# The column term of the attention logits as two more columns of the q product, with the q tiles ahead of the exponentials

## What is computed

```python
h = maximum(layernorm(x), 0)                       # 512 x 256
Xw = h @ Wv + bv
sj = Xw @ aw[:256]; si = Xw @ aw[256:]             # one number per node each
e = leaky_relu(sj[None, :] + si[:, None] + ab, 0.2)
alpha = adj * exp(e)
T = alpha / (sum(alpha, -1) + 1e-12)
out = relu(h@Wk0 + T h@Wk1 + T T h@Wk2 + biases)   # q = h @ Wk2 is made first
```

## Time and profile before

| | |
|---|---|
| median of 3 runs | 1858.39 us (1857.15 to 1858.89) |
| profiled execution: its span | 1856.2 us |
| median less the profiled span | 2.2 us |
| mean granted clock of PE | 0.924 of 2.4 GHz |
| turns with both halves | 15 |

### The profile page before, as it was taken

One profiled execution on the slowest core, in us unless ns is written; L12 is line 12 of the kernel. 1 busy time (PEld: TensorE's weight loads), 2 busy tenths in 40 slices (PEclk: granted clock), 3 DMA queues, 4 the chain that ended last, 5 costly groups with the idle time before them and its releaser, 6 DMA issues.

```text
span 1856.2 us, 27152 instructions
## 1 busy us (share of the span) xinstructions
PE 1539.5 (83%) x9334; PEld 1185.5 (64%) x9334; DVE 1339.2 (72%) x3050; ACT 787.7 (42%) x1271; POOL 274.1 (15%) x167
## 2 busy tenths in 40 slices
PE   4587988979798898988989898897989789798855
PEld 3486665757667575766757676675767667576632
DVE  5666868777686877768687776868767686876623
ACT  2224436353453635335353533535353363534432
POOL 1101120111202011120201112020111201012010
PEclk9788999989899898989989898998989899898977
DMA  5013131132313203231320323123031312313030
GB/s 158 12 52 80 52 100 65 38 78 73 90 51 97 67 34 79 73 90 51 86 78 34 79 73 90 51 73 91 23 90 63 101 51 61 83 43 80 22 81 11
DMA packets 80806, 125.52 MB, mean 68 GB/s; under 512 B 10176, under 2 KB 29184, under 8 KB 80768
## 3 DMA queue, kind: packets, MB, share of 16 engines
q1 hardware_dynamic: 80768, 125.02, 24.0%
HBM read 66.27 MB, written 8.39 MB: 40 GB/s over the span
## 4 chain that ended last, share of the span: by engine, by line
PE 56%; DVE 16%; issue 13%; ACT 6%; POOL 5%; SPq 2%; DMA 1%; DVEq 0%; POOLq 0%; ACTq 0%
PE ring_f L1023 32%; PE ring_b L1023 16%; DVE att L969 6%; PE pv_acc L1289 2%; PE ring_f L1179 1%; POOL xp_s L445 1%; POOL xf L428 1%; POOL xf L426 1%; PE ring_f L1209 1%; DVE rows L898 1%; ACT att L596 1%; DVE rows L879 1%; PE ring_f L1121 1%; ACT uz L472 1%; DVE hf L850 1%
## 5 line engine op out<-in xcount | busy, mean ns | idle before, releaser
L1023 PE MATMUL ring_f<-m,inc_n 128*128 128x256 f32 x2048 | 324.2, 288 | 17.0 <-POOL m L418 14.4
L969 DVE TENSOR_TENSOR att<-ring_b,at 128x1024 f32<-128x1024 f32 x256 | 299.2, 1216 | 31.1 <-PE ring_b L1023 30.5
L575 ACT ACTIVATE att<-att 128x1024 f32<-128x1024 f32 x256 | 263.7, 1066 | 100.3 <-DVE att L969 94.4
L1023 PEld LDWEIGHTS ring_f<-m,inc_n 128*128 128x128 f32 x2048 | 289.2, 194 | 25.4 <-issue 21.0
L1023 PE MATMUL ring_b<-stk_c,stk_p 96*128 96x512 f32 x512 | 183.7, 477 | 61.1 <-DMA stk_c<-xc_s 44.5
L1023 PE MATMUL ring_f<-m,inc_t 128*128 128x256 f32 x1024 | 210.3, 284 | 14.5 <-DVE m L728 14.5
L1023 PE MATMUL ring_f<-w,uz 128*128 128x256 f32 (+1 forms) x896 | 188.1, 333 | 13.0 <-DVE uz L721 8.4
L1023 PEld LDWEIGHTS ring_b<-stk_c,stk_p 96*128 96x128 f32 x512 | 97.7, 217 | 147.3 <-issue 70.1
L407 POOL TENSOR_TENSOR rstd_f<-var_f,mhalf 128x4 f32<-128x4 f32 x48 | 48.5, 1010 | 933.2 <-DVE var_f L715 933.2
L1023 PEld LDWEIGHTS ring_f<-w,uz 128*128 128x128 f32 x896 | 151.6, 191 | 34.0 <-DVE uz L721 14.8
L1023 PEld LDWEIGHTS ring_f<-m,inc_t 128*128 128x128 f32 x1024 | 160.4, 191 | 17.7 <-DVE m L728 17.7
(11 more groups left out here) (163 smaller groups left out, 2656.7 us busy)
## 6 DMA issues: line engine op xcount, KB each, us to landing
stk_p<-xp_s SPq DMA_DIRECT2D x192, 128.0 KB, 2.4
stk_c<-xc_s SPq DMA_DIRECT2D x192, 128.0 KB, 2.3
rows<-in_adjT SPq DMA_DIRECT2D x16, 1024.0 KB, 5.3
adj_n<-in_adj SPq DMA_DIRECT2D x16, 1024.0 KB, 8.5
at<-in_adjT SPq DMA_DIRECT2D x16, 1024.0 KB, 5.2
x_in<-in_x SPq DMA_DIRECT2D x16, 512.0 KB, 3.5
out_x<-xb SPq DMA_DIRECT2D x16, 512.0 KB, 2.9
wrow<-in_adj SPq DMA_DIRECT2D x16, 256.0 KB, 6.0
```

Source lines behind the costliest of these rows:

```text
L575: act.activation(v, v, ACT.Tanh).then_inc(tanh_made.sem, 1)
L969: dve.tensor_tensor(att[:, u % 2, 2 * half:2 * half + 2], pair(tile)[:], at[:, t].unsqueeze(1).broadcast_to([P, 2, N]), ALU.mult)\
L1023: ins = pe.matmul(dst, lhsT, rhs, start=(first and n == 0), stop=(last and n == len(pairs) - 1), skip_group_check=True)
```

## The change

It does three things. The column term no longer comes from VectorE: two columns (the vector and 0.2 times the vector) are put behind the 256 of `wq`, so that each q tile has two more columns that hold si for its 128 nodes, and VectorE adds a constant pair `cst2` to them (128x2, from PSUM). The q tiles stand ahead of sj in the numbering and on PE, and their copies and subtractions ahead of the exponentials on ScalarE and VectorE. The set-up makes the two columns from a product of 2 columns in place of a row of 256.

```diff
-        wq = sb("wq", [P, 2, DT, D], F32R)
+        wq = sb("wq", [P, 2, DT, D + 2], F32R)
...
-        T_M, T_U, T_CONV, T_ZT, T_XW, T_M2, T_Y, T_HT, T_SJ, T_Q, T_TT, T_R, T_X2 = (
-            0, 2, 4, 8, 12, 14, 16, 18, 20, 21, 25, 29, 31)
+        T_M, T_U, T_CONV, T_ZT, T_XW, T_M2, T_Y, T_HT, T_Q, T_SJ, T_TT, T_R, T_X2 = (
+            0, 2, 4, 8, 12, 14, 16, 18, 20, 24, 25, 29, 31)
...
                 if i == 0:
-                    act.wait_ge(si_made.sem, si_made.after(g, 2))
+                    act.wait_ge(si_made.sem, si_made.after(g, NT))
...
-                step(dve.tensor_copy(v2_bc[:], ring_b[1][:, 0, 0:D]))
+                for c in range(DT):
+                    step(dve.tensor_copy(v2_c[:, c, 0:1], ring_b[1][:, 0, 2 * c:2 * c + 1]))
+                    step(dve.tensor_scalar(v2_c[:, c, 1:2], ring_b[1][:, 0, 2 * c:2 * c + 1], SLOPE, None, ALU.mult),
+                         now=True)
+                split(wq[:, 0, :, D:D + 2], wq[:, 1, :, D:D + 2], v2_c[:])
...
-            def f_si(g):
-
-                dve.wait_ge(h_made.sem, h_made.after(g, 2))
-                for i in range(NT):
-                    ins = dve.scalar_tensor_tensor(rows[:, i, 0:D], hf[:, i], 1.0, v2_bc[:], ALU.mult, ALU.mult,
-                                                   accum_out=si[:, 0, i:i + 1])
-                dve_f.link(ins)
-                here(dve_f, g)
-                dve.tensor_scalar(si[:, 0], si[:, 0], cst, None, ALU.add).then_inc(si_made.sem, 1)
-                dve.wait_ge(si_made.sem, si_made.after(g, 1))
-                dve.tensor_scalar(si[:, 1], si[:, 0], SLOPE, None, ALU.mult).then_inc(si_made.sem, 1)
...
                 dve.wait_ge(hi_made.sem, hi_made.after(g, H_Q + i + 1))
+                dve.tensor_tensor(si[:, i], ring_f[tile % 3][:, D:D + 2], cst2[:], ALU.add).then_inc(si_made.sem, 1)
...
-                products(ps[:, 0:D], pairs).then_inc(full.sem, 1)
+                products(ps[:, 0:D + 2], pairs).then_inc(full.sem, 1)
...
-                    (1, k_xc), (0, f_m2), (0, f_y), (1, k_scores, 0), (0, f_hT), (1, k_scores, 1), (0, f_sj),
-                    (0, f_q, 0), (1, k_attend, 0), (1, k_scores, 2), (1, k_attend, 1), (1, k_scores, 3),
-                    (1, k_attend, 2), (1, k_scores, 4), (0, f_q, 1), (0, f_q, 2), (1, k_attend, 3), (0, f_q, 3),
+                    (1, k_xc), (0, f_m2), (0, f_y), (1, k_scores, 0), (0, f_hT), (1, k_scores, 1), (0, f_q, 0),
+                    (0, f_q, 1), (1, k_attend, 0), (1, k_scores, 2), (0, f_q, 2), (0, f_q, 3), (0, f_sj),
+                    (1, k_attend, 1), (1, k_scores, 3), (1, k_attend, 2), (1, k_scores, 4), (1, k_attend, 3),
```

More of the change, by code:

```diff
@@ L139, in graph_layers @@
         b2_bc = sb("b2_bc", [P, D])
-        v2_bc = sb("v2_bc", [P, D])
+        v2_c = sb("v2_c", [P, DT, 2])
         ident = sb("ident", [P, P])
+        cst2 = sb("cst2", [P, 2])
         prm = sb("prm", [P, 24])
@@ L152, in graph_layers @@
         dn = sb("dn", [P, NT])
-        si = sb("si", [P, 2, NT])
+        si = sb("si", [P, NT, 2])
         rs = sb("rs", [P, NT])
@@ L211, in graph_layers @@
         z_made = Signal(sem("z_made"), NT)
-        si_made = Signal(sem("si_made"), 2)
+        si_made = Signal(sem("si_made"), NT)
         max_made = Signal(sem("max_made"), NT)
@@ L221, in graph_layers @@
         drained_b = Signal(sem("drained_b"), 20)
-        dve_f = Chain(sem("dve_f"), 18)
+        dve_f = Chain(sem("dve_f"), 17)
         dve_b = Chain(sem("dve_b"), 6)
@@ L252, in graph_layers @@
         SET_FIRST = 25
-        SET_DONE = 42
+        SET_DONE = 48
         BE_LINK = 5
@@ L520, in f_exp @@
                 if i == 0:
-                    act.wait_ge(si_made.sem, si_made.after(g, 2))
+                    act.wait_ge(si_made.sem, si_made.after(g, NT))
                     act.wait_ge(full.sem, full.after(g, T_SJ + 1))
-                act.activation(rows[:, i], ring_f[T_SJ % 3][:], ACT.Exp, bias=si[:, 0, i:i + 1], scale=1.0)
+                act.activation(rows[:, i], ring_f[T_SJ % 3][:], ACT.Exp, bias=si[:, i, 0:1], scale=1.0)
                 if i >= 2:
                     act.wait_ge(max_made.sem, max_made.after(g, i - 1))
-                act.activation(exp_s(i), ring_f[T_SJ % 3][:], ACT.Exp, bias=si[:, 1, i:i + 1],
+                act.activation(exp_s(i), ring_f[T_SJ % 3][:], ACT.Exp, bias=si[:, i, 1:2],
                                scale=SLOPE).then_inc(exp_made.sem, 1)
@@ L688, in set_up_rest @@
                     split(v1[:, 0, c], v1[:, 1, c], ring_b[0][:, 1, c * P:(c + 1) * P])
-                step(dve.tensor_copy(v2_bc[:], ring_b[1][:, 0, 0:D]))
+                for c in range(DT):
[3 more added lines that the diff above has]
+                split(wq[:, 0, :, D:D + 2], wq[:, 1, :, D:D + 2], v2_c[:])
                 step(dve.tensor_scalar(cst, pv_acc[:, 0:1], ab_c, None, ALU.add), now=True)
-                step(dve.tensor_tensor(cst, pv_acc[:, 1:2], cst, ALU.add))
+                step(dve.tensor_tensor(cst2[:, 0:1], pv_acc[:, 1:2], cst, ALU.add), now=True)
+                step(dve.tensor_scalar(cst2[:, 1:2], cst2[:, 0:1], SLOPE, None, ALU.mult))
                 assert n_set[0] == SET_DONE, n_set[0]
@@ L1004, in turn @@
                     (0, f_xw, 0), (1, k_keep), (0, f_xw, 1), (0, f_m2), (1, k_xc), (0, f_y), (0, f_stats2),
-                    (0, f_norm1), (1, k_unit, 0), (0, f_si), (0, f_hT), (1, k_unit, 1), (0, f_alpha, 0), (0, f_q, 0),
-                    (1, k_unit, 2), (0, f_alpha, 1), (1, k_unit, 3), (0, f_alpha, 2), (1, k_unit, 4),
-                    (0, f_alpha, 3), (0, f_sums), (0, f_q, 1), (0, f_trans), (0, f_q, 2), (0, f_q, 3), (0, f_tt),
+                    (0, f_norm1), (1, k_unit, 0), (0, f_hT), (1, k_unit, 1), (0, f_q, 0), (0, f_q, 1),
+                    (1, k_unit, 2), (0, f_q, 2), (0, f_q, 3), (0, f_alpha, 0), (1, k_unit, 3), (0, f_alpha, 1),
+                    (0, f_alpha, 2), (1, k_unit, 4), (0, f_alpha, 3), (0, f_sums), (0, f_trans), (0, f_tt),
                     (1, k_unit, 5), (-1, f_stats0), (1, k_unit, 6), (1, k_unit, 7), (-1, f_norm0), (0, f_r, 0),
@@ L1041, in set_up @@
                                                                for f in range(DT)])
-                products(ring_b[1][:, 0, 0:D], [(xp_n[:, 3, f * P:(f + 1) * P], wvt[:, f]) for f in range(DT)])
+                for c in range(DT):
+                    products(ring_b[1][:, 0, 2 * c:2 * c + 2], [(wvt[:, f, c * P:(c + 1) * P], xp_n[:, 3, f * P:f * P + 2])
+                                                                for f in range(DT)])
                 products(pv_acc[:, 0:2], [(ones, bva)]).then_inc(set_pe, 1)
@@ L1187, in f_sj @@
             def f_sj(g):
-                if not seen(g, 1):
-                    pe.wait_ge(set_dve, SET_DONE)
                 ps = bank(g, T_SJ)
                 for c in range(DT):
-                    pe.wait_ge(drained.sem, drained.after(g, drained_at(T_HT + c)))
                     v = slice(c * N, (c + 1) * N)
@@ L1197, in f_q @@
             def f_q(g, i):
+                if i == 0 and not seen(g, 1):
+                    pe.wait_ge(set_dve, SET_DONE)
                 ps = bank(g, T_Q + i)
+                if i == 0:
+                    pe.wait_ge(drained.sem, drained.after(g, drained_at(T_HT + 1)))
                 pairs = []
```

8 lines of the change are left out of this document (4 added, 4 removed).

## The result

The changed kernel takes 1892.49 us (1890.83 to 1896.57, 4 runs), before 1858.64 in the same session: ratio 1.0185, 95% interval 1.0172 to 1.0197, slower by 34 us. The profiled execution has a span of 1889.0 us, 32.8 more than before, at a mean granted clock of 0.907 (0.924 before).

A forecast was written before the change was run, and what follows sets the result against it. In the rewritten stretch PE led the chain of waits, then mostly VectorE. Delay 1.84 plus clock fall 2.2 minus give-back 0.8 made 3.2 us a turn, over 15 turns +49 us: 1907 us, range 1847 to 1916.

The forecast's parts named there:

- the forecast itself: The main case for the whole kernel's time: 1895 to 1916 us, chance 0.54.
- clock holds: Rival: no further clock fall, the delay remains; 0.3 to 1.8 us a turn, 1863 to 1885 us, chance 0.18.
- the third fall: One more drop of PE's clock each turn, just ahead of the dense work at 961.2, costing 2.2 us a turn.
- the give-back: Turns of another length lie otherwise against the clock's falls; 0.8 us a turn subtracted, ends 0 and 1.8.
- the first turn: Without a back graph, its q tiles ahead of sj cost about what the row sums saved; taken as 0.
- The row sums are covered: Row sums (1.86 us of VectorE a turn) are not in the chain; PE runs scores 1 meanwhile.
- sj comes late: Behind the q tiles on PE, sj is full at 947.8 instead of 943.46, and the exponentials wait for it.
- The division 1.84 us later: VectorE's balance for the end of L898: -1.86 +0.40 +0.70 +2.60 = +1.84 us a turn.
- the thin one: PE stretch between the attends, such as 953.4 to 956.8, busy only 1.4 of 3.4 us, ahead of a clock fall.
- turns of 111 to 113.5 us: Sign expected in the trace after: length of a turn, where settled turns took 109.23 us.
- Faster: Rival: VectorE stays the one bound of the stretch, its waiting does not grow; 1831 to 1847 us, chance 0.14.
- Absorbed: Rival: turns settle at 109.23 us again, the delay is paid once or twice; 1857 to 1862 us, chance 0.08.

The follow-up runs named there:

- no_row_sums: The kernel before, its order kept, without the four row products of the column term (that sum is left out); 1855.76 us, ratio 0.9979.
- order_only: The changed kernel's order with the old arithmetic: four row sums on VectorE again, q with 256 columns; 1913.79 us, ratio 1.0288.
- warm_no_row_sums: The kernel before with 48 idle matmuls a turn in PE's three holes and without the four row products; 1816.49 us, ratio 0.9769.
- after_filled: The changed kernel with 18 idle matmuls a turn in the holes that the q tiles left on PE; 1883.46 us, ratio 1.0127.
- dense_4: The kernel before with 4 idle matmuls a turn in a dense stretch of PE, ahead of the m2 products; 1859.86 us, ratio 0.9999.
- dense_16: The kernel before with 16 idle matmuls a turn in a dense stretch of PE, ahead of the m2 products; 1876.54 us, ratio 1.0090.

## Why the prediction was right, step by step

The direction and its cause held, and 1892.5 us lies in the range of 1847 to 1916. It lies just under the 1895 to 1916 of the forecast itself, between it and the rival "clock holds", and my value was 15 us too high. Four terms were mis-sized, and in part they cancel: over the program the delay came out 5 us smaller than I had it, the third fall 26 smaller, the give-back 9 smaller, and the first turn 5 larger. That I was not further off is luck.

**The row sums are covered.** Right. no_row_sums takes them away for 3.5 us. What I did not see: they are covered only in the old order, and there only while PE runs scores 1 at 1.2 GHz. order_only shows them on the chain in the new order, warm_no_row_sums in the old one with the clock held.

**sj comes late.** Right. I had sj full 4.3 us later; the first exponential starts 3.8 and 4.8 us later, with waits in front of the exponential (1.01 us, predicted 1.1) and of alpha 0 (1.42, predicted 1.47) where I put them.

**The division 1.84 us later.** By its start, which I had 1.65 us later, 1.0 and 2.0 us were measured, in the mean 1.49. The waits of VectorE that I listed add up to 3.70 us (my balance says 3.9; with 3.7 it gives 1.64, the delay of the start); the long turn has 3.68, the short one 2.75. The shorter turns are those in which q 0 and q 1 ran mostly at 2.4 GHz, which I had laid out at 1.2.

**The third fall.** It is there in all settled turns but one, behind a stretch that stands about where I had put the thin one. Its price was the term furthest off: 0.45 us in the table, 0.5 to 0.6 by after_filled, against 2.2. I had let it fall just ahead of the dense work behind the division. It comes earlier, 1198.7 in the long turn above, and lies over scores and attend 4 (in the short turn attend 3 too), which wait anyway, and over the transposes of T, which alternate with ScalarE and VectorE; the clock is back by 1205.6, ahead of wk at 1206.84. The Trainium skill's rule of long gaps (TensorE: Matmul & The Clock Gate, "Why this matters for your kernels") would have no fall here, the longest idle spell ahead of it being 2.01 us; the trace disagrees. That page's other remark, in "A second HAM failure mode: psum-queue depth-cycling", that frequent short idle spells also bring the clock down, agrees with it.

**The give-back of 0.8 us.** Small here: 0.17 in the rest of the turn. It is real where the change is small (dense_4). A part of it may be in the short turns' 1.0 above; no run separates it.

**The first turn, taken as 0.** Wrong, it cost 4.7 us. There is no other graph to fill PE there, and PE ran at 1.2 GHz (granted clock 0.50): the four q tiles stood ahead of sj, and the first exponential started 10.73 us behind the transposes of h in place of 5.65.

```profile
86.76 5.50 PE L1018 MATMUL ring_f<-wq,uz 128*128 128x258 f32 x24 [1.50 <-DVE uz L727]
```

I had weighed them against row sums that were off the chain in that turn as well: without them (no_row_sums) its division stands 13.40 us behind the transposes, with them 13.39.

So 15 x (1.49 + 0.45 - 0.17) + 4.7 is 31 us of the 33 between the two profiled spans; the rest lies in turns unlike the four of the table, the first ones above all. Of the signs that I had named, the turns of 111 to 113.5 us came only in part: they are 110.0 to 111.9.

**Rivals.** "Faster" is out: VectorE was not the one bound. "Absorbed" is a true mechanism (0.5 us a turn in dense_4, 0.9 in dense_16) that this change outran. "Clock holds" is out by the trace, though its 1863 to 1885 us are the nearest of the rivals, since the fall turned out cheap.

## What to carry to other kernels

Before you take work off an engine, look whether the chain passes through it; here 23 us of VectorE were worth 3.5, and became worth 20 when PE's clock no longer led, or 21 in the new order. When a term is moved into a product that is already made, count what must now be ready before its first reader: the exponentials needed one tile and now need five. Where PE idles in short spells and its clock falls ahead of critical work, idle matmuls in those spells can pay for themselves, if they are enough: 48 a turn gave 23 us here, 30 gave 14.

## What the runs showed of the hardware that I had not expected

A loop with falls of the clock in it can settle to a fixed turn and swallow a small change whole: 0.48 us of PE work a turn on the chain moved the time by 0.3 us in 1859 (ratio 0.9999, 0.9990 to 1.0008), while 1.92 us a turn moved it by 17. In such a kernel a test of a small edit says little of what the edit costs.

The changed kernel settled not to one turn but to two that alternate, 110.0 to 110.4 and 111.8 to 111.9 us, with the clock returning 3.3 to 3.8 us behind the transposes of h in one and 5.9 to 6.3 us behind them in the other.

48 matmuls of 256 columns a turn, more work for the engine that is the busiest, made the kernel 23 us faster (granted clock 0.975 in place of 0.924).
